# Three-layer graph network with segment maximum: earlier patch gathers, leads of the last groups kept on chip, carry by chunk, a new head

## The reference, cut to what matters

```python
h = jnp.maximum(_layernorm(x, axis=-1), 0.0)
def _sage_conv(x, src, dst, Wl, bl, Wr):
    agg = jax.ops.segment_max(x[src], dst, num_segments=x.shape[0])
    agg = jnp.where(jnp.isfinite(agg), agg, 0.0)
    return agg @ Wl + bl + x @ Wr
for Wl, bl, Wr in layers:
    h = leaky_relu(_sage_conv(h, src, dst, Wl, bl, Wr), 0.01)
return x + h
```

## Time and profile before

| What | Value |
|---|---|
| Median of 3 runs | 6193.24 us (6192.94 to 6194.87) |
| The profiled execution | 6178.24 us, its span 6176.4 us |
| Busy: POOL, DVE, PE, ACT | 4607.9, 2882.1, 695.5, 227.9 us |
| First gather of layer 1 starts | 46.03 us |
| Last column gathers of layers 1, 2, 3 start | 2003.82, 4044.07, 6088.31 us |
| HBM read, written | 555.13 MB, 533.14 MB |

### The profile page before, as it was taken

The page is one execution under the profiler, slowest core; times in us unless marked ns, Lnnn a source line. Parts: engine busy times, 40 slices in busy tenths (PEclk is TensorE's granted clock), DMA queues, the critical chain, the costliest instruction groups (busy, mean ns, idle before and its releaser), DMA issues. The chain is left out here.

```text
span 6176.4 us, 24426 instructions
## 1 busy us (share of the span) xinstructions
PE 695.5 (11%) x2214; PEld 399.1 (6%) x2214; DVE 2882.1 (47%) x3614; ACT 227.9 (4%) x664; POOL 4607.9 (75%) x4878
## 2 busy tenths in 40 slices
PE   0111111111100780000000000057000000000003
PEld 0000000000000340000000000034000000000002
DVE  4333333333333555555555555565555555555556
ACT  1000000000000110000000000011000000000001
POOL 6777777777777677777777777767777777777776
PEclk8555555555555655555555555565555555555556
DMA  4333333333333576666666666667666666666665
GB/s 129 107 107 108 105 107 107 107 107 107 107 104 107 171 236 210 209 210 209 210 211 210 211 209 210 209 205 246 210 210 210 210 211 208 212 208 210 209 210 171
DMA packets 435669, 1088.94 MB, mean 176 GB/s; under 512 B 101413, under 2 KB 154154, under 8 KB 435642
## 3 DMA queue, kind: packets, MB, share of 16 engines
q0 software_dynamic: 206976, 530.17, 30.4%
q1 hardware_dynamic: 203706, 537.55, 23.4%
q10 hardware_dynamic: 24960, 20.95, 1.1%
HBM read 555.13 MB, written 533.14 MB: 176 GB/s over the span
## 5 line engine op out<-in xcount | busy, mean ns | idle before, releaser
L365 POOL DMA_INDIRECT ring<-features,stage x4692 | 4439.4, 946 | 1451.3 <-issue 1406.8
L656 DVE TENSOR_TENSOR ring<-banks,ring 128x1024 f32<-128x1024 f32 (+1 forms) x1173 | 1226.5, 1046 | 3066.8 <-DMA ring<-features,stage 3049.3
L635 DVE TENSOR_TENSOR banks<-ring,banks 128x1024 f32<-128x1024 f32 (+1 forms) x1173 | 1232.2, 1050 | 37.6
L869 PE MATMUL banks<-ident,ring 128*128 128x128 f32 x20 | 5.0, 428 | 3763.5 <-DVEq L668 3763.5
L843 PE MATMUL banks<-dst_low,own 128*128 128x394 bf16 x200 | 99.5, 498 | 1459.8 <-DVE own L619 1459.8
L869 PEld LDWEIGHTS banks<-ident,ring 128*128 128x128 f32 x20 | 3.9, 222 | 3764.9 <-DVEq L668 3538.1
L827 PE MATMUL banks<-wr,h_turned 128*128 128x256 f32 (+1 forms) x490 | 204.0, 559 | 95.9 <-ACT h_turned L965 95.9
L1009 ACT ACTIVATE agg<-zeros 128x512 f32<-128x512 f32 x75 | 47.3, 630 | 3957.4 <-PE banks L901 3957.4
L390 POOL DMA_INDIRECT ring<-running_max_log,end_row x147 | 141.6, 964 | 60.5 <-issue 43.9
L624 DVE COPY stage<-edges 128x8 int32 (+1 forms) x588 | 129.1, 220 | 84.8 <-DVE banks L635 25.8
L829 PE MATMUL banks<-b,ones 1*128 1x256 f32 (+1 forms) x294 | 141.9, 579 | 0.0
(11 more groups left out here) (104 smaller groups left out, 560.8 us busy)
## 6 DMA issues: line engine op xcount, KB each, us to landing
running_max_log<-ring SPq DMA_DIRECT2D x782, 512.0 KB, 3.2
running_max_log<-ring SPq DMA_DIRECT2D x391, 256.0 KB, 2.3
ring<-features,stage POOLq DMA_INDIRECT x4692, 2.8
h_in<-features ACTq DMA_DIRECT2D x98, 128.0 KB
features<-h_out SPq DMA_DIRECT2D x48, 256.0 KB, 2.2
ring<-x SPq DMA_DIRECT2D x5, 640.0 KB, 10.4
features<-ring SPq DMA_DIRECT2D x5, 640.0 KB, 3.7
h_in<-features ACTq DMA_DIRECT2D x49, 64.0 KB
```

Of the source, the lines that this page charges most:

```text
L365: pool.indirect_dma_start(ring[:, c * w:(c + 1) * w], None, tables[l], bass.IndirectOffsetOnAxis(ap=stage[:, b, u:u + 1].bitcast(U32), axi ...
L635: dve.tensor_tensor(sum_ps[:, 0:CHAINS * w].rearrange("p (h f) -> p h f", h=CHAINS), group(g - 1).rearrange("p (h f) -> p h f", h=CHAINS), ...
L656: dve.tensor_tensor(group(g), sum_ps[:, 0:CHAINS * w], group(g), ALU.max).then_inc(turn, 1)
```

## The change

Six edits, in one diff:

1. **Log in two parts.** The last 12 columns of each partition (`LATE`, groups 10 to 12 of the last step) go to a region of their own. The row for nodes without edges moves from the end to row 0, and the early rows begin at row 1 with a stride of 1552 rows for each partition. `end_rows` computes the new row numbers (12 instead of 11 small steps).
2. **Patch gathers.** POOL waits only for the log of blocks 0 to 4 before them; the wait for all blocks now stands behind `patch_stored`. A run whose lead ends in the late part reads row 0.
3. **Leads of the late groups.** `late_lead` is set to the lowest float before the last step. `keep_lead` copies, under a mask in PSUM (`lead_goes_on`), a whole group into it: once for each of the groups 10, 11 and 12, in every layer. The first two stand in front of the wait for block 6, the third behind the last group. One more maximum joins it with the gathered rows.
4. **Landing of block 5 in the last step.** Its first four columns and its last four have a wait each (`late_landed`).
5. **Carry by chunk.** Semaphores count per chunk of 128 features; `back_ps` is laid out by chunk, and the last maximum is one instruction for each chunk.
6. **Head.** Chunks of 6, 11, 12, 12 and 8 tiles (49, not 50), all input loads on SP's queue, one overlapping load of `dst` in place of one load and eight of single words, weights behind the stores of the table, the order check as one `tensor_tensor_reduce` behind the normalising, a small activation at the start of ACT, the last three tiles of the last chunk on DVE, indices staged from `src` ahead of the branch, restart values from the differences of the check.

```diff
-TAIL_TILES = 10
+CHUNKS = (6, 11, 12, 12, 8)
+ACT_TILES = (4, 8, 9, 8, 3)
+POOL_TILES = (2, 3, 3, 4, 2)
+VARS_AFTER = (4, 8, 6, 3)
+RECIPROCAL_AFTER = 4
...
-    NO_EDGES = P * COLS
-    PATCHED = NO_EDGES + 1
+    LATE_BLOCK = BLOCKS - 2
+    LATE = LAST - LATE_BLOCK * BLOCK_COLS
+    EARLY = COLS - LATE
+    EARLY_GROUPS, LATE_GROUPS = EARLY // CHAINS, LATE // CHAINS
+    NO_EDGES, EARLY_ROWS = 0, 1
+    LATE_ROWS = EARLY_ROWS + P * EARLY
+    PATCHED = LATE_ROWS + P * LATE
...
+        lead_goes_on = banks[:, 5, RING_COLS:RING_COLS + LATE].bitcast(I32).rearrange("p (g h) -> p g h", h=CHAINS)
...
-                            ).then_inc(landed[b], DMA)
+                            ).then_inc(late_landed if last and b == LATE_BLOCK and u >= CHAINS else landed[b], DMA)
...
-                for b in reversed(range(BLOCKS)):
+                pool.wait_ge(prep_done, PREP)
+                pool.wait_ge(empty_stored, DMA * len(widths))
+                for b in range(LATE_BLOCK):
                     pool.wait_ge(logged[b], LOGGED[b] * (l + 1))
-                pool.wait_ge(prep_done, PREP)
                 for h in range(CHAINS):
                     pool.indirect_dma_start(
-                        patch[:, h * w:(h + 1) * w], None, logs[w][0:NO_EDGES, :],
+                        patch[:, h * w:(h + 1) * w], None, logs[w][0:LATE_ROWS, :],
...
                 pool.wait_ge(patch_stored, DMA * (l + 1))
-                pool.wait_ge(empty_stored, DMA * len(widths))
+                for b in reversed(range(BLOCKS)):
+                    pool.wait_ge(logged[b], LOGGED[b] * (l + 1))
...
-            for s in range(TAIL_STEPS):
+            for s in range(HEAD_STEPS):
                 statistics(s)
-                if s == 0:
-                    check_order()
-                else:
-                    normalise(s - 1)
-            normalise(TAIL_STEPS - 1)
+            normalise(HEAD_STEPS - 1)
+            for k in range(rest.start, rest.stop):
+                dve.tensor_scalar(h0_all[:, k, :], x_all[:, k, :], rstd[:, k:k + 1], shift[:, k:k + 1],
+                                  ALU.mult, ALU.add).then_inc(h0_last_scaled, 1)
+            dve.tensor_scalar(h0_all[:, rest, :], h0_all[:, rest, :], 0.0, None, ALU.max).then_inc(h0_last_done, 1)
+            dve.wait_ge(dst_loaded, DMA)
+            dve.tensor_tensor_reduce(out=falls, in0=dst_w[:, :, 0:RUN], in1=dst_runs, scale=1.0, scalar=0.0,
+                                     op0=ALU.subtract, op1=ALU.max, accum_out=highest_fall[:, :])
+            dve.tensor_scalar(disorder[:, :], highest_fall[:, :], 0.0, None, ALU.is_gt)
+            dve.wait_ge(src_loaded, DMA)
+            stage_first()
...
-            dve.tensor_tensor(restart_turns[:, :, 1:RUN], dst_runs[:, :, 1:RUN], dst_runs[:, :, 0:RUN - 1],
-                              ALU.not_equal).then_inc(prep_done, 1)
-            dve.tensor_scalar(restart_turns[:, :, 1:RUN], restart_turns[:, :, 1:RUN], LOWEST, None, ALU.mult)
+            dve.tensor_scalar(restart_turns[:, :, 1:RUN], falls[:, :, 1:RUN], 0.0, LOWEST,
+                              ALU.not_equal, ALU.mult).then_inc(prep_done, 1)
...
+                def keep_lead(g):
+
+                    dve.wait_ge(lead_kept, KEPT * l + g + 1)
+                    dve.copy_predicated(late_lead[:, 0:CHAINS * w].rearrange("p (h f) -> p h f", h=CHAINS),
+                                        lead_goes_on[:, g, :].unsqueeze(2).to_broadcast([P, CHAINS, w]),
+                                        group(LAST // CHAINS - LATE_GROUPS + g).rearrange("p (h f) -> p h f", h=CHAINS)
+                                        ).then_inc(lead_kept, 1)
...
+                            if last and g == groups - 1:
+                                for e in range(LATE_GROUPS - 1):
+                                    keep_lead(e)
...
+                        elif last and b == LATE_BLOCK:
+                            dve.wait_ge(turn, carried + 2 * g + 1)
+                            dve.wait_ge(late_landed, DMA * CHAINS * (l + 1))
...
+                dve.memset(late_lead[:, :], LOWEST).then_inc(lead_kept, 1)
                 scan_step(STEPS - 1, True, False)
...
                 for c in range(kc):
+                    dve.wait_ge(carry_turned, CHUNKS_TO[l] + c + 1)
                     dve.tensor_tensor_scan(carry_scan[:, c, 1:RUNS + 1], pass_row[:, :],
...
-                dve.wait_ge(incoming_turned, l + 1)
                 dve.wait_ge(patch_landed, DMA * CHAINS * (l + 1))
-                dve.tensor_tensor(patch[:, 0:CHAINS * w], patch[:, 0:CHAINS * w], back_ps[:, 0:CHAINS * w],
-                                  ALU.max).then_inc(patched, 1)
+                dve.wait_ge(lead_kept, KEPT * (l + 1))
+                dve.tensor_tensor(patch[:, 0:CHAINS * w], patch[:, 0:CHAINS * w], late_lead[:, 0:CHAINS * w],
+                                  ALU.max).then_inc(lead_joined, 1)
+                for c in range(kc):
+                    dve.wait_ge(incoming_turned, CHUNKS_TO[l] + c + 1)
+                    dve.tensor_tensor(patch_rows[:, :, c * P:(c + 1) * P], patch_rows[:, :, c * P:(c + 1) * P],
+                                      back_ps[:, c * RUNS:(c + 1) * RUNS].rearrange("p (h f) -> p h f", h=CHAINS),
+                                      ALU.max).then_inc(patched, 1)
...
+            for s in range(3):
+                load_x(s)
+            sp.dma_start(dst_w, dst_seen).then_inc(dst_loaded, DMA)
+            for s in range(3, HEAD_STEPS):
+                load_x(s)
+            sp.dma_start(src_runs.rearrange("p (h j) -> p h j", h=CHAINS),
+                         src.rearrange("(h p) j -> p h j", p=P)).then_inc(src_loaded, DMA)
```

More of the change, by code:

```diff
@@ L39, in gnn_program @@
     RUN = src.shape[1]
+    edge_dst = dst[1:1 + src.shape[0] * RUN].rearrange("(r j) -> r j", j=RUN)
+    dst_seen = bass.AP(dst.tensor, 0, [[RUN, P], [P * RUN, CHAINS], [1, RUN + 2]])
     COLS = CHAINS * RUN
@@ L43, in gnn_program @@
     LAST = COLS - (STEPS - 1) * RING_COLS
-    TAIL_STEPS = TILES // TAIL_TILES
+    HEAD_STEPS = len(CHUNKS)
+    FROM = [sum(CHUNKS[:s]) for s in range(HEAD_STEPS + 1)]
     PAIRS = TILES // 2
@@ L48, in gnn_program @@
     assert PAIR_TILES[-1] == 1 and PAIR_TILES[-2] == 2
-    assert TILES % TAIL_TILES == 0
+    assert FROM[-1] == END_TILES
+    assert all(a + p == c for a, p, c in zip(ACT_TILES[:-1], POOL_TILES, CHUNKS))
     assert PAIRS < STEPS and RUN + 3 <= BANK and CHAINS % 2 == 0
@@ L234, in gnn_program @@
         LAYERS = len(shapes)
[L235 to L238, removed]
+        LOADS = 6
+        CONSTS = 14 + 2 * CHAINS
+        PREP = 22 + 2 * CHAINS
+        ENDS = 12
+        KEPT = 1 + LATE_GROUPS
         N_WEIGHTS = 3 * LAYERS * DMA
+        CHUNKS_TO = [sum(k for k, _ in shapes[:l]) // P for l in range(LAYERS + 1)]
         PER_OUT = PAIRS // STORES * DMA
@@ L246, in log_block @@
             w = shapes[l][0]
-            body = logs[w][0:P * COLS, :].rearrange("(p c) f -> p (c f)", p=P)
-            return body[:, bass.ds((step * BLOCKS + b) * (BLOCK_COLS * w) + at * w, columns * w)]
-        def run_neighbours(runs):
[L252 to L257, removed]
+            if isinstance(step, int) and step == STEPS - 1 and b >= LATE_BLOCK:
+                late = logs[w][LATE_ROWS:PATCHED, :].rearrange("(p c) f -> p (c f)", p=P)
+                at += (b - LATE_BLOCK) * BLOCK_COLS
+                return late[:, at * w:(at + columns) * w]
+            early = logs[w][EARLY_ROWS:LATE_ROWS, :].rearrange("(p c) f -> p (c f)", p=P)
+            return early[:, bass.ds((step * BLOCKS + b) * (BLOCK_COLS * w) + at * w, columns * w)]
+        def run_neighbours(runs):
+            own_runs = runs.rearrange("(h p) j -> p h j", p=P)
+            pairs = [(prev_last[1:P, :], own_runs[0:P - 1, :, RUN - 1]),
+                     (prev_last[0:1, 1:CHAINS], own_runs[P - 1:P, 0:CHAINS - 1, RUN - 1]),
+                     (next_first[0:P - 1, :], own_runs[1:P, :, 0]),
+                     (next_first[P - 1:P, 0:CHAINS - 1], own_runs[0:1, 1:CHAINS, 0])]
             return pairs
@@ L1072 @@
     edges = inputs["src"].shape[0]
-    group = P * TAIL_TILES
-    rows = -(-nodes // group) * group
+    rows = -(-nodes // (2 * P)) * 2 * P
     runs = CHAINS * P
@@ L1088 @@
         "src": filled(np.asarray(inputs["src"]), runs * run, 0),
-        "dst": filled(np.asarray(inputs["dst"]), runs * run, NO_NODE),
+        "dst": np.concatenate([[-1], filled(np.asarray(inputs["dst"]), runs * run, NO_NODE).ravel(), [1 << 24]]
+                              ).astype(np.int32),
     }
```

236 lines of the change are left out of this document (130 added, 106 removed).

## The result

| | Kernel before | Changed kernel |
|---|---|---|
| Median of 5 runs | 6193.42 us (6192.94 to 6194.87) | 6166.49 us (6165.47 to 6166.67) |
| Profiled execution | 6178.24 us | 6166.19 us |
| Its span | 6176.4 us | 6164.4 us |

The ratio is 0.9957, with a 95% interval of 0.9945 to 0.9968: 26.9 us less. The forecast was 6166.9. The traced executions, however, are only 12.0 us apart, where the forecast had 26.3. That gap of 14 us is the first thing to explain. The traced execution of the kernel before (6178.24 us) lies outside the range of its five timed ones (6192.94 to 6194.87), that of the changed kernel (6166.19) inside.

The account below looks back on a forecast made before the run. POOL's 4692 column gathers, one each 1.25 us, were taken to bound the kernel. Head minus 16.5, collision plus 3.7, layer ends minus 13.5 give 26.3 off the median 6193.24: 6166.9 us, range 6158 to 6180 (8 in 10).

Parts of the forecast that it names:

- the collision: Head: DVE's preparation, now under the first gathers, costs them 7.0 us in place of 3.3, plus 3.7.
- Layer 1, minus 4.3: Layer end, 128 features: patch gathers start earlier, their landing ends the wait, patch store at 2012.85 in place of 2017.14.
- Layers 2 and 3, minus 4.6 each: Layer ends, 256 features: patch gathers start 6.4 us earlier, DVE's chain ends it, patch store at 6099.1 in place of 6103.70.
- block 5 has landed, 6083.31 + 2.8: Layer 3's end: group 11 may start at 6086.1, 2.8 us after block 5's gather at 6083.31.
- the rival with 2.8 us: Layer ends, 256 features: masked copies of 2.8 us or more each win nothing there; total 6180 to 6184; 8%.
- Head, first gather at 29.5: Head: the first column gather starts at 29.5 us in place of 46.03, minus 16.5.
- the stores end it: Head: table stores landing at 29.0 to 29.3, not DVE's indices at 27.7, set the first gather at 29.5.
- 3.34 of 4.16 us: Head: loss rate of gathers beside DVE's preparation, from one long gather before the change, applied to 8.7 us of exposure.
- its full exclusion: Head: by the skill's rule alone all 8.7 us beside DVE's preparation are lost, the sum 1.7 us smaller.
- The wholly shut-out stream: Head: only one gather goes out before the restart pass ends at about 42; total gain 22.0, 6171.2 us; 20%.
- Slower stores of the log: Layers 2 and 3: the log's new layout makes stores 2.3 times as long, 80 us more, 6247 us; 4%.
- The better case: Head: gathers and DVE's preparation do not collide, total minus 30 us or more; 8%.

Follow-up runs that it names:

- the two comparisons of medians: Changed kernel against the kernel before: the five runs of the result, then both again unchanged on one chip, 6155.66 us against 6182.34, 26.4 less.
- the pair of kernels: Changed kernel with four extra 128x512-bank copies of 128x1564 on DVE under the first gathers, 6156.36 us; or four sums over as many elements instead, 6154.00 us.
- all_three: Changed kernel with group 10's store held until block 5 landed, its masked copy in DVE's idle time, POOL out of the head's last chunk: 6152.26 us, 0.9952.
- its three neighbours: Changed kernel with four extra DVE copies (6156.36 us), with four extra DVE sums (6154.00), or without POOL's tiles in the head's last chunk (6154.34).
- ends_only: The kernel before with edits 1 to 5, without the new head: 6170.60 us, ratio 0.9982.

## Why the prediction was right

**The number.** 6166.9 was forecast, 6166.49 measured; the sum was 26.3, the parts in the traces give 25.7, the two comparisons of medians 26.9 and 26.4. That the sum was made in one trace and carried over to the median was the step that mattered. That the total ends within 1 us is luck in part: by the traces the first gather missed its term by 2.7 us, the layer ends theirs by 2.7 together, and the collision was 4.8 better than forecast. The forecast for the profiled execution, 6151.9, was wrong by 14 us (6166.19): the trace of before was of an execution 15 us under its median, that of the changed kernel lies at its median. Of the signs named for being wrong, one came: its pace, about 1.2525 us a gather in that trace, was not 1.248 (and the 1.248 was low from the start: layer 3 of the kernel before has 1563 steps in 1953.8 us, 1.250 each).

**Layer 1, minus 4.3:** measured 4.32, ended by the landing of the patch rows. Right in size and mechanism.

**Layers 2 and 3, minus 4.6 each:** measured 3.4 and 3.1. The mechanism was right (patch gathers 1.25 behind the last column gather, DVE's chain the next bound). The term that was mis-sized is "block 5 has landed, 6083.31 + 2.8". The earlier maximum of group 10 sends its store of 512 KB out 1.7 us after group 9's (6073.91 and 6072.22), into the last gathers of the block, which land 1.7 us later. I had followed the split wait on DVE and not on SP's queue. The masked copy was 1.32 us, not 1.25. In layer 1 it takes 0.72 us for 128x512, where the plain one takes 0.73, so its mask with a step of 0 costs nothing: the rival with 2.8 us is refuted.

**Head, first gather at 29.5:** it was 32.20. POOL's tiles of the last chunk took 2.63 us beside DVE's tiles and the check, where I gave them ACT's length, and the store went out at 26.82, not 24.7. Yet without POOL's tiles the store went out at 24.83, as forecast, and the first gather still started at 31.81. The step that failed is "the stores end it": the forecast had a term for DVE's way from the flag (2.19 us) and none for POOL's, which was hidden before. POOL's took 5.4 to 5.9 us; why it takes so long stays open.

**Collision, plus 3.7:** it was a gain of 1.1. Two gathers lost 1.45 and 1.0 us, together 2.5, where 7.0 was forecast and 3.5 is what the kernel before loses. The rate of "3.34 of 4.16 us" came from one gather under two long passes back to back. With the copies it is 1.6 of 4.0 us. It also helped that the first gather came 2.7 us later, when a part of the preparation was over. For the head 12.8 was forecast and 14.9 came; the surplus of 2.1 covers most of what the layer ends fell short by. The Trainium skill's rule (SBUF — State Buffer, "Who interferes with whom") names the right kinds of instruction: copies stretch the gathers and reductions don't, as the pair of kernels shows. The sum made from its full exclusion did not hold: beside four copies back to back (37.51 to 41.51) a whole gather began and ended (38.91 to 40.62), so the reckoning by it (a gain 1.7 us smaller) was further off than the rate from the row.

**Rivals.** The wholly shut-out stream is refuted by the head's trace (five gathers started before 40 us). Slower stores of the log: all_three and its three neighbours, which have the new layout, keep the pace of the kernel before, and ends_only, which has it too, is 11.5 us faster; refuted. The better case, no collision and 30 us or more, did not come either: two gathers were stretched.

## What to carry to other kernels

When a kernel is bound by a steady stream, add up what stands outside it, compare streams by a late member (the 13th gather, not the first), and check the pace on both sides before reading a difference of two traces: 3 ns in 4692 steps hid half of this gain, in one trace on either side. When a wait is split so that an engine may start earlier, follow every transfer that the earlier start lets go, and look where it lands. Beside gathers issued by GpSimd, keep on VectorE the kinds of instruction that don't stretch them, and price the ones that do by a row in which they stand alone. When several terms of a sum miss in opposite directions, a total that fits says little for the terms.

## What the runs showed that I had not expected

- The pace of POOL's gathers differs between traces of one program: 1121 against 1120 in 1400 us for the kernel before, 1118 against 1120 for the changed one, and 1121 for all_three, which has the changed kernel's layout. The kernel before had a median of 6193 us in the first comparison, 6182 on two other chips, and 7024 on one where SP was 10 to 13 stores behind at the layer ends.
- With a store of 512 KB issued 1.7 us behind another, the gathers beside it land 1.7 us later, though the transfer engines are busy for 0.66 of the time on average (4200 to 6000 us of the changed kernel).
- POOL's first gather comes 5.4 to 5.9 us after the flag it branches on, though its queue is past the branch after 1.8 us in the changed kernel (26.46 to 28.2). Two instruction loads lie in between. DVE works again 1.7 to 2.4 us after the flag.
